# A transformer block on one core: weight differences made once and kept in DRAM, in place of being remade at each use

## The chip, the core and the metric

The kernel runs on one core of a Trainium2 chip. Its engines run side by side and meet through semaphores: TensorE (PE: matrix products and transposes), VectorE (DVE), ScalarE (ACT), GpSimd (POOL) and SyncE (SP), whose queue issues almost all transfers between DRAM and the on-chip memory. The metric is the device time of one execution in microseconds (us), lower is better. A change of under 0.2% cannot be told from none here.

## What is computed

64 sequences of 64 positions and 256 features go through four layers: cross attention with a gate (L0), cross attention with 16 heads and a GELU feed-forward block (L1), and two layers (2 and 3) that have two sets of weights each, `v` and `l`. A mask `vm` chooses per position which set is used. The change is in their feed-forward blocks:

```python
vm = expert_mask(token_type_ids)[..., None]      # True where this and the next type are 1
mi = rms_norm(hidden_states, ln_post_attn_w)
v_out = silu(mi @ v_gate) * (mi @ v_up) @ v_down
l_out = silu(mi @ l_gate) * (mi @ l_up) @ l_down
hidden_states = hidden_states + where(vm, v_out, l_out)
```

The weights are 256 x 688 (gate, up) and 688 x 256 (down), float32.

## The kernel before

**The product with a difference.** For every position the kernel multiplies by `l`, and adds the product of `v - l` with the activations masked by `vm`: where the mask is 0 the second part vanishes, where it is 1 it turns `l` into `v`. For this input only positions 48 to 63 of a sequence have a mask that can be 1 (`late`, a branch chosen on the chip at the start), so the second product covers 128 of 512 columns.

**Groups, streams, turns.** The 64 sequences make 8 groups of 512 positions. Two groups are in work at once, stream a (0) and stream b (1), and there are 4 turns of two groups. While one stream is in attention, which has long chains over all engines, the other is in a feed-forward block, which is mostly TensorE work. At the very end stream b's last feed-forward block has nothing beside it.

**The feed-forward steps.** 688 hidden features are 6 tiles (`j` 0 to 5, five of 128 and one of 48). A tile has the steps `g` (gate product, PE; lines 1358 and 1364), `silu` (DVE and POOL), `u` (up product, the same lines, then DVE 1817 to 1837 and POOL) and `down` (lines 1375, 1385).

**The ring.** The weights of a tile (a chunk: 768 KB, `l` and `v` of gate, up and down) are loaded anew at each use into one of 5 slots of `w_ring`, by six transfers on SP's queue (lines 937 to 939). GELU chunks (`f1`) use the same ring. A slot is reloaded when the last product of its chunk is done. There are 96 feed-forward chunks: 4 turns x 2 streams x 2 layers x 6.

**The step `weigh`.** After a chunk has landed, GpSimd turns its `v` part into `v - l` in place: three subtractions (line 1908 twice, line 1909), and PE's `g` waits for the third. GpSimd also normalises the attention's probabilities (`prob`, line 1861), builds block-diagonal keys (1891, 1899), and takes a part in the rotation (`rot`, 1884) and in the masks (1878, 1916, 1924).

**The planner.** The order of steps on each engine is computed when the kernel is built: `schedule` takes the steps in a nominal order (`global_order`), and puts next the one that could start first by its table of assumed costs (`parts`), by what it must follow (`follows`), and by the free banks and ring slots (`room`). Each engine then runs its list strictly in order. Where the plan leaves PE idle before a step, `PAUSES` gives a number of filler products (line 982: a 128x512 bf16 product into the bank that the step will overwrite), issued in the step's place in the order, before the step's own waits. SP's order (`transfers`) is by planned time too.

**The norm.** RMS norms take their reciprocal root on DVE by nine dependent operations on 128x2 or 128x4 elements (lines 1711 to 1731); the step `spread` (PE, line 1217) waits for the last.

Of the kernel before, what the change touches and what calls it, by code (L numbers as in the profile page):

```python
# [163 lines left out]


def attention_lane(n):
    return q_stage(n)[0] + [(when + q_stage(n)[1], *step) for when, *step in attention_stage(n)[0]]


def global_order():  # L170
# [22 lines left out]
    then((1, TURNS - 1, finish, (0, 0), (3, 3)))  # L193
    return order

# [150 lines left out]


def accumulation(token):

    return token[:3] + (token[3:4] if token[0] == "down" else ())  # L350
# [7 lines left out]
def schedule(nominal):  # L358
# [33 lines left out]
    def inputs(token):  # L392
        if token not in ready_at:
            step, s, turn, *where = token
            latest = 0.0
            for engine, t, name, *at in follows(step, turn, where):
                other = (name, s if name != "table" else 0, t, *at)
                when = over.get(other) if engine is None else end.get((other, engine))
                if when is None:
                    return None  # L400
                latest = max(latest, when)
            ready_at[token] = latest
        return ready_at[token]
# [8 lines left out]
    def room(token):  # L412
# [3 lines left out]
        if step == "weigh":  # L416
            return slot()
        if step == "l1h" and where[0] % 2 == 0:
            there, free = slot(), banks(1)
            return None if there is None or free is None else max(there, free)  # L420
# [52 lines left out]
    while True:  # L473
# [26 lines left out]
        if pieces[k][2] is None and token not in orders_set:  # L500

            orders_set.add(token)
            heads[step, s].pop()
            if step == "weigh":
                chunks.append((("ffn", s, turn, *where), ("down", s, turn, *where)))
            if step == "l1h" and where[0] % 2 == 0:
                chunks.append((("f1", s, turn, where[0] // 2), ("w2", s, turn, where[0] + 1)))
            for j, (other, _, follow) in enumerate(pieces):
                if follow is None and j != k:
                    waiting.setdefault(key_of(step, s, other), []).append((token, j, at))  # L510
# [54 lines left out]
def transfers():  # L565

    found = [(BEGIN[token, "SP"], token) for token in ORDER["SP"] if token[0] == "store" or token[2]]
    for chunk, n in CHUNKS.items():
        found.append((END[CHUNK_ENDS[n - SLOTS], "PE"] if n >= SLOTS else -1.0, ("chunk", *chunk)))
    return [token for _, token in sorted(found, key=lambda v: v[0])]  # L570

# [49 lines left out]
def xattn_kernel(nc, a, out):  # L621
    ctx = ExitStack()

    def sb(name, shape, dt=F32):
# [132 lines left out]
    g_ready, th_ready, silu_ready, h_ready = (pair(name, 2 * FT) for name in ("g_ready", "th_ready", "silu_ready", "h_ready"))  # L757
    weighed, sv_ready, hv_late, hv_early, down_done = (pair(name, 2 * FT) for name in ("weighed", "sv_ready", "hv_late", "hv_early", "down_done"))
    w_weighed = sem("w_weighed")
    out_ready = pair("out_ready", 2)  # L760
# [73 lines left out]
    def sums(token):  # L834

        return [banks[BANK["sum", m, accumulation(token)]] for m in range(DT)]

    def chunk(*key):

        n = CHUNKS[key]  # L840
        count = sum(16 * (2 if c[0] == "f1" else 6) for c, m in CHUNKS.items() if m <= n and m % SLOTS == n % SLOTS)
        return w_ring[:, n % SLOTS, :], (chunk_loaded[n % SLOTS], count)

    def f1_weights(ring):
        return (ring[:, 0:512].rearrange("p (k n) -> p k n", k=DT), ring[:, 512:1024].rearrange("p (t d) -> p t d", t=2))

    def ffn_weights(ring):
# [46 lines left out]
    with nc.Block() as block:  # L894
        @block.sync
        def _(q):
# [20 lines left out]
            def load_chunk(*key):  # L917
                ring, _ = chunk(*key)
                n = CHUNKS[key]
                if n >= SLOTS:  # L920
                    step, s, turn, *where = CHUNK_ENDS[n - SLOTS]
                    if step == "w2":
                        q.wait_ge(*w2_done[s].at(turn, where[0] + 1))
                    else:
                        q.wait_ge(*down_done[s].at(turn, FT * (where[0] - 2) + where[1] + 1))
                here = chunk_loaded[n % SLOTS]
                if key[0] == "f1":
# [7 lines left out]
                into, down = ffn_weights(ring)  # L935
                for e in "lv":
                    q.dma_start(into["g"][e][:, :, 0:rows], tiles(a[f"L{layer}_{e}_gate"])[:, :, j * P:j * P + rows]).then_inc(here, 16)
# [24 lines left out]
            for step, *where in ORDER["SP"][SLOTS:]:  # L962
                if step == "load":
                    load(*where)
                elif step == "chunk":
                    load_chunk(*where)
                elif step == "store":
                    s, turn = where
# [3 lines left out]
            for s in range(STREAMS):  # L972
                q.wait_ge(*stored[s].at(TURNS, 0))

        @block.tensor
        def _(pe):
# [150 lines left out]
            def stages(every):  # L1127
                for token in ORDER["PE"]:
# [212 lines left out]
                    if step in ("g", "u"):  # L1341
                        n, j = where
                        rows = P if j < FT - 1 else FR
                        ring, _ = chunk("ffn", s, turn, n, j)
# [501 lines left out]
        def _(pool):  # L1846
# [3 lines left out]
            for token in ORDER["POOL"]:  # L1850
# [49 lines left out]
                if step == "weigh":  # L1900
# [8 lines left out]
                    G_.tensor_tensor(down["v"][0:rows, :], down["v"][0:rows, :], down["l"][0:rows, :], ALU.subtract).then_inc(weighed[s].sem, 1)  # L1909
                if step == "silu":  # L1910
# [57 lines left out]
```

## Time and profile before

| | us |
|---|---|
| median of 3 runs | 2689.42 (2686.3 to 2690.03) |
| the profiled execution: time | 2684.68 |
| its span, first to last instruction | 2682.8 |
| PE busy | 2560.8, 95% |
| DVE busy | 1534.7, 57% |
| ACT busy | 1222.7, 46% |
| POOL busy | 1155.9, 43% |
| transfers, mean | 41 GB/s |

The mean granted TensorE clock is 0.993 of full. Busy time of PE includes the filler products. Times within the span are from its start. The turns begin at about 0, 660, 1318 and 1977 us.

### The profile page before, as it was taken

The page shows a single profiled execution, that of the slowest core. Times are in us where ns is not written, and L with a number is a line of the kernel's source. Part 1 is how long each engine was busy: PE and PEld are TensorE (multiplying, and loading weights), DVE is VectorE, ACT ScalarE, POOL GpSimd, SP SyncE. Part 2 cuts the span into 40 slices and gives each one's busy share as a digit, 9 for nine tenths or more (in the row PEclk, how much of TensorE's full clock was granted, in tenths as well). Part 3 has the DMA queues.
Part 4 walks back from the last instruction along what each step waited for, and adds up shares of the span by engine and source line. Part 5 has one row for each costly group of instructions (what it writes and reads, how often), then busy time and mean ns, then how long its engine had stood idle before and what let it go on. Part 6 is the DMA issues. An engine that isn't in the chain of part 4 may idle for free.

```text
span 2682.8 us, 54240 instructions
## 1 busy us (share of the span) xinstructions
PE 2560.8 (95%) x20342; PEld 1554.7 (58%) x20342; DVE 1534.7 (57%) x3448; ACT 1222.7 (46%) x4274; POOL 1155.9 (43%) x1242
## 2 busy tenths in 40 slices
PE   6999999999999999999999999999999999999998
PEld 3556556665565656566555565665656556566565
DVE  2537556766434646776644464677644456467763
ACT  2335444644333635464433362654544346265462
POOL 0025265665211527656410342765641034267564
PEclk9999999999999999999999999999999999999999
DMA  8010011112201011121220101112121000120211
GB/s 211 1 32 2 22 44 48 41 41 72 72 2 32 2 41 40 32 58 31 70 68 1 32 2 52 38 28 60 29 72 60 9 25 2 52 60 10 55 41 44
DMA packets 171100, 109.61 MB, mean 41 GB/s; under 512 B 31764, under 2 KB 168408, under 8 KB 170712
## 3 DMA queue, kind: packets, MB, share of 16 engines
q1 hardware_dynamic: 166384, 105.82, 14.2%
q8 instruction: 167, 2.74, 0.4%
q10 hardware_dynamic: 4456, 0.29, 0.2%
q14 instruction: 93, 0.76, 0.1%
HBM read 101.87 MB, written 4.19 MB: 40 GB/s over the span
## 4 chain that ended last, share of the span: by engine, by line
PE 82%; DVE 11%; POOL 2%; issue 2%; ACT 1%; ACTq 1%; DMA 0%; SPq 0%; DVEq 0%
PE bank L1358 10%; PE bank L1375 6%; PE bank L1081 6%; PE bank L995 5%; PE bank L1244 4%; PE bank L1251 4%; PE bank L1263 4%; PE bank L1272 4%; PE bank L1364 3%; PE bank L1116 2%; PE bank L1298 2%; PE bank L1098 2%; PE bank L1057 2%; PE bank L1224 2%; PE bank L1070 2%
## 5 line engine op out<-in xcount | busy, mean ns | idle before, releaser
L1861 POOL TENSOR_TENSOR Ebuf<-Ebuf,row_rcp 128x512 f32<-128x512 f32 (+1 forms) x328 | 345.8, 1060 | 797.4 <-DVE row_rcp L1684 796.3
L1463 ACT ACTIVATE Ebuf<-bank,minus_max 128x64 f32<-128x64 f32 x1312 | 392.4, 334 | 39.8 <-DVE minus_max L1668 39.5
L1668 DVE TENSOR_REDUCE minus_max<-bank 128x8 f32<-128x512 f32 (+1 forms) x328 | 219.8, 673 | 161.2 <-PE bank L1070 81.2
L1463 ACT ACTIVATION_READ_ACCUMULATOR Ebuf<-bank,minus_max 128x1 f32 x1312 | 297.4, 227 | 0.0
L1472 ACT ACTIVATE PT<-bank 128x512 f32<-128x512 f32 (+1 forms) x328 | 192.6, 601 | 152.5 <-PE bank L1081 151.0
L1081 PE MATMUL bank<-ident,Ebuf 128*128 128x128 f32 x1296 | 201.5, 283 | 9.9 <-POOL Ebuf L1861 9.4
L1081 PEld LDWEIGHTS bank<-ident,Ebuf 128*128 128x128 f32 x1296 | 146.4, 143 | 64.5 <-issue 39.2
L1358 PE MATMUL bank<-xs_a,w_ring 128*128 128x512 f32 (+1 forms) x384 | 172.2, 611 | 7.7 <-POOL w_ring L1909 7.3
L1358 PE MATMUL bank<-xs_b,w_ring 128*128 128x512 f32 (+1 forms) x384 | 169.1, 602 | 5.9 <-POOL w_ring L1909 3.9
L1456 ACT ACTIVATE Ebuf<-Ebuf 128x512 f32<-128x512 f32 x160 | 102.0, 638 | 101.6 <-DVE Ebuf L1673 99.5
L1908 POOL TENSOR_TENSOR w_ring<-w_ring 128x256 f32<-128x256 f32 x192 | 131.9, 708 | 0.0
L1673 DVE TENSOR_TENSOR Ebuf<-bank,minus_max 128x512 f32<-128x512 f32 x160 | 110.7, 692 | 16.9 <-DVE minus_max L1668 0.5
L1682 DVE TENSOR_REDUCE row_sum<-Ebuf 128x8 f32<-128x512 f32 x160 | 107.9, 675 | 8.6 <-ACT Ebuf L1456 7.8
L982 PE MATMUL bank<-causal_bf,ident_bf 128*128 128x512 bf16 x414 | 109.3, 384 | 0.0
L1684 DVE RECIPROCAL row_rcp<-row_sum 128x8 f32<-128x8 f32 (+1 forms) x328 | 65.4, 200 | 70.6 <-ACT Ebuf L1463 64.5
L1358 PEld LDWEIGHTS bank<-xs_a,w_ring 128*128 128x128 f32 (+1 forms) x384 | 59.4, 180 | 67.7 <-issue 65.1
L1358 PEld LDWEIGHTS bank<-xs_b,w_ring 128*128 128x128 f32 (+1 forms) x384 | 59.1, 179 | 66.6 <-issue 64.3
L1375 PE MATMUL bank<-arena_a,w_ring 128*128 128x512 f32 (+1 forms) x192 | 94.2, 613 | 1.7 <-DVE arena_a L1833 1.7
L1375 PE MATMUL bank<-arena_b,w_ring 128*128 128x512 f32 (+1 forms) x192 | 92.9, 606 | 2.7 <-DVE arena_b L1833 2.7
L1878 POOL TENSOR_TENSOR xs_a<-xs_a,masks_a 128x192 f32<-128x192 f32 (+1 forms) x48 | 36.2, 774 | 133.4 <-DVE xs_a L1745 133.4
L1817 DVE SCALAR_TENSOR_TENSOR arena_b<-arena_b 128x512 f32<-128x512 f32 (+1 forms) x48 | 42.7, 889 | 76.2 <-ACT arena_b L1581 76.0
L1899 POOL TENSOR_TENSOR arena_b<-arena_b,head_rows 128x512 f32<-128x512 f32 x64 | 65.5, 1056 | 42.5 <-PE bank L1070 28.9
(325 smaller groups left out, 5599.6 us busy)
## 6 DMA issues: line engine op xcount, KB each, us to landing
w_ring<-in_L_W SPq DMA_DIRECT2D x64, 256.0 KB, 3.0
w_ring<-in_L_l_gate SPq DMA_DIRECT2D x80, 128.0 KB, 2.2
w_ring<-in_L_l_up SPq DMA_DIRECT2D x80, 128.0 KB, 2.3
w_ring<-in_L_l_down SPq DMA_DIRECT2D x80, 128.0 KB, 2.2
w_ring<-in_L_v_gate SPq DMA_DIRECT2D x80, 128.0 KB, 2.4
w_ring<-in_L_v_up SPq DMA_DIRECT2D x80, 128.0 KB, 2.4
w_ring<-in_L_v_down SPq DMA_DIRECT2D x80, 128.0 KB, 2.5
arena_a<-in_x SPq DMA_DIRECT2D x4, 512.0 KB
```

Source lines behind the costliest of these rows:

```text
L982: mm(b[:, :].rearrange("p (h s) -> p h s", h=8), ident_bf[:, :], causal_bf[:, :].unsqueeze(1).broadcast_to([P, 8, S]), start=True, stop=True)
L995: mm(b, w_l[k], src_l[k], start=(k == 0), stop=(not every and k == DT - 1))
L1081: last = nc.tensor.transpose(b[:, c * P:(c + 1) * P], Ebuf[:, u % UNITS, c * P:(c + 1) * P], ident[:, :])
L1358: mm(to, of["l"][:, k, 0:rows], st.xn[:, k, :], start=(k == 0), stop=(not every and k == DT - 1))
L1375: mm(acc[m][:, :], w["l"][0:rows, m * P:(m + 1) * P], st.hid_l[0:rows, j % 2, :], start=(j == 0), stop=(not every and j == FT - 1), skip_g ...
L1463: last = A(Ebuf[:, u % UNITS, cell], bank(token)[:, cell], ACT.Exp, bias=minus_max[:, u % UNITS, c:c + 1], accum_out=row_sum[:, u % UNITS, ...
L1472: A(PT[:, t % 2, 0:width(key) * S], bank(token)[:, 0:width(key) * S], ACT.Copy).then_inc(pt_ready, 1)
L1668: V.reduce_max(minus_max[:, u % UNITS, 0:g], cells(bank(token)[:, 0:g * S]), AX_X, negate=True).then_inc(maxed, 1)
L1673: V.tensor_tensor(cells(Ebuf[:, u % UNITS, 0:g * S]), cells(bank(token)[:, 0:g * S]), minus_max[:, u % UNITS, 0:g].unsqueeze(2).broadcast_ ...
L1682: V.reduce_sum(row_sum[:, u % UNITS, 0:g], cells(Ebuf[:, u % UNITS, 0:g * S]), AX_X).then_inc(summed, 1)
L1861: G_.tensor_tensor(v, v, row_rcp[:, n % 3, 0:g].unsqueeze(2).broadcast_to([P, g, S]), ALU.mult).then_inc(probs_ready, 1)
L1908: G_.tensor_tensor(rare, rare, other, ALU.subtract)
```

## The change

`weigh` stays only for the first use of each chunk: stream a, turn 0, layers 2 and 3, 12 of 96. After it SP's queue writes the differences of that chunk to a DRAM tensor `differences` (step `keep`). Every later use loads `l` by three transfers as before, and the three differences by one transfer of 384 KB (three for the 48-row tile), and PE's `g` waits for these transfers themselves. A load of a difference waits until its `keep` has landed, and a slot whose difference is being kept is not reloaded before. The planner drops the other 84 `weigh` steps, and claims the ring slot of such a chunk when it places `g`.

```diff
+def first_use(token):
+    return token[1:3] == (0, 0)
...
-    return order
+    return [(when, token) for when, token in order if token[0] != "weigh" or first_use(token)]
...
+def begins_chunk(token):
+    return token[0] == "g" and not first_use(token) or token[0] == "l1h" and token[3] % 2 == 0
...
             for engine, t, name, *at in follows(step, turn, where):
+                if name == "weigh" and not first_use(token):
+                    continue
...
-        if step == "l1h" and where[0] % 2 == 0:
+        if begins_chunk(token):
             there, free = slot(), banks(1)
...
-            if step == "weigh":
-                chunks.append((("ffn", s, turn, *where), ("down", s, turn, *where)))
             if step == "l1h" and where[0] % 2 == 0:
                 chunks.append((("f1", s, turn, where[0] // 2), ("w2", s, turn, where[0] + 1)))
+            elif step == "weigh" or begins_chunk(token):
+                chunks.append((("ffn", s, turn, *where), ("down", s, turn, *where)))
...
+    for token in ORDER["POOL"]:
+        if token[0] == "weigh":
+            found.append((END[token, "POOL"], ("keep", *token[1:])))
     return [token for _, token in sorted(found, key=lambda v: v[0])]
...
+    scratch = nc.dram_tensor("differences", (2 * FT, P, 3, DT * P), F32).ap()
...
+    kept = [sem(f"kept{k}") for k in range(SLOTS)]
...
+                    if step == "down" and first_use(CHUNK_ENDS[n - SLOTS]):
+                        q.wait_ge(*kept_at(*where))
...
-                for e in "lv":
+                if not first_use(key):
+                    q.wait_ge(*kept_at(layer, j))
+                    for dst, src in zip(rarer(rare_share(ring), j), rarer(scratch[FT * (layer - 2) + j], j)):
+                        q.dma_start(dst, src).then_inc(here, 16)
+                for e in "lv" if first_use(key) else "l":
                     q.dma_start(into["g"][e][:, :, 0:rows], ...).then_inc(here, 16)
...
+                elif step == "keep":
+                    n, j = where[2:]
+                    ring, _ = chunk("ffn", *where)
+                    q.wait_ge(weighed, FT * (n - 2) + j + 1)
+                    for dst, src in zip(rarer(scratch[FT * (n - 2) + j], j), rarer(rare_share(ring), j)):
+                        q.dma_start(dst, src).then_inc(kept_at(n, j)[0], 16)
...
                         if step == "g":
-                            pe.wait_ge(*weighed[s].at(turn, FT * (n - 2) + j + 1))
+                            pe.wait_ge(*((weighed, FT * (n - 2) + j + 1) if first_use(token) else there))
```

The planner's orders change with this. The lines of the changed kernel are 51 higher in this part of the file: 1358 becomes 1409, 1364 becomes 1415, 982 becomes 1033.

PE, second turn, the start of stream a's feed-forward block of layer 2. L1298 is stream b's value projection of layer 2; L1358 and L1364 with `xs_a` are one gate or up product. Before, around the gate product of tile 1:

```order
L1298 MATMUL bank7<-w2_l_qkv,xs_b 128x256 x2
L1298 MATMUL bank7<-w2_v_qkv,xs_b 128x256 x2
L1358 MATMUL bank4<-xs_a,w_ring 128x512 x2
L1364 MATMUL bank4<-xs_a,w_ring 128x8x16 x2
L1298 MATMUL bank0<-w2_l_qkv,xs_b 128x256 x2
L1298 MATMUL bank0<-w2_v_qkv,xs_b 128x256 x2
```

The same product now, the second of the two that stand first:

```order
L1409 MATMUL bank3<-xs_a,w_ring 128x512 x2
L1415 MATMUL bank3<-xs_a,w_ring 128x8x16 x2
L1409 MATMUL bank4<-xs_a,w_ring 128x512 x2
L1415 MATMUL bank4<-xs_a,w_ring 128x8x16 x2
L1259 MATMUL bank7<-ones,sq 128x1 x4
L1033 MATMUL bank2<-causal_bf,ident_bf 128x512 x2
L1409 MATMUL bank2<-xs_a,w_ring 128x512 x2
L1415 MATMUL bank2<-xs_a,w_ring 128x8x16 x2
```

Gate 1 has moved from between stream b's value projections to right behind gate 0, ahead of stream b's norm (L1259).

PE, last turn, the start of stream b's last feed-forward block; L982 is the filler. Before:

```order
L982 MATMUL bank2<-causal_bf,ident_bf 128x512 x4
L1358 MATMUL bank2<-xs_b,w_ring 128x512 x2
L1364 MATMUL bank2<-xs_b,w_ring 128x8x16 x2
L982 MATMUL bank0<-causal_bf,ident_bf 128x512 x6
L1358 MATMUL bank0<-xs_b,w_ring 128x512 x2
L1364 MATMUL bank0<-xs_b,w_ring 128x8x16 x2
L1358 MATMUL bank5<-xs_b,w_ring 128x512 x2
L1364 MATMUL bank5<-xs_b,w_ring 128x8x16 x2
```

The same place now:

```order
L1033 MATMUL bank3<-causal_bf,ident_bf 128x512 x4
L1409 MATMUL bank3<-xs_b,w_ring 128x512 x2
L1415 MATMUL bank3<-xs_b,w_ring 128x8x16 x2
L1409 MATMUL bank1<-xs_b,w_ring 128x512 x2
L1415 MATMUL bank1<-xs_b,w_ring 128x8x16 x2
L1033 MATMUL bank0<-causal_bf,ident_bf 128x512 x2
L1409 MATMUL bank0<-xs_b,w_ring 128x512 x2
L1415 MATMUL bank0<-xs_b,w_ring 128x8x16 x2
```

Six fillers between gate 0 and gate 1 are gone, two came ahead of the up product. Over the whole branch that this input takes, the fillers go from 414 to 385: by turn 118, 92, 94, 110 before, and 111, 93, 94, 87 now.

POOL, second turn, beside the first place: the rotation of stream b (`cos_sin`) and its keys (`head_rows`). Before:

```order
L1884 TENSOR_TENSOR arena_b<-arena_b,cos_sin 128x512 x3
L1908 TENSOR_TENSOR w_ring<-w_ring 128x256 x2
L1909 TENSOR_TENSOR w_ring<-w_ring 128x256
L1884 TENSOR_TENSOR arena_b<-arena_b,cos_sin 128x512
L1891 TENSOR_TENSOR arena_b<-arena_b,head_rows 128x2x256 x2
L1908 TENSOR_TENSOR w_ring<-w_ring 128x256 x2
L1909 TENSOR_TENSOR w_ring<-w_ring 128x256
```

Now:

```order
L1929 TENSOR_TENSOR xs_b<-xs_b,masks_b 128x8x48 x2
L1975 TENSOR_TENSOR arena_a<-arena_a,masks_a 128x8x48
L1935 TENSOR_TENSOR arena_b<-arena_b,cos_sin 128x512 x4
L1942 TENSOR_TENSOR arena_b<-arena_b,head_rows 128x2x256 x6
L1912 TENSOR_TENSOR Ebuf<-Ebuf,row_rcp 128x512
```

The subtractions on `w_ring` stood between the rotation and the keys, and are gone.

## Rows read from the trace of the kernel before

**Rows 1.** The page, parts 1 and 4: busy time; the chain that ended last.

```profile
PE 2560.8 (95%) x20342; PEld 1554.7 (58%) x20342; DVE 1534.7 (57%) x3448; ACT 1222.7 (46%) x4274; POOL 1155.9 (43%) x1242
...
PE 82%; DVE 11%; POOL 2%; issue 2%; ACT 1%; ACTq 1%; DMA 0%; SPq 0%; DVEq 0%
```

**Rows 2.** Busy time by stretch, the second turn and the last.

```profile
core 0: us, PE busy (x) PEld busy (x) DVE busy (x) ACT busy (x) POOL busy (x), PEclk, DMA share, GB/s
660.00:1318.00 658.00, 635.65 (x5073) 387.05 (x5072) 383.04 (x856) 305.38 (x1068) 286.47 (x309) 0.99 0.14 38
1977.00:2683.00 706.00, 676.80 (x5248) 409.19 (x5246) 394.50 (x876) 314.32 (x1083) 304.14 (x336) 1.00 0.13 37
```

**Rows 3.** Waits of PE: who for whom, us in total, times, longest.

```profile
PE bank L1217 <- DVE norm_a L1731: 25.3, 18, 2.0
PE bank L1217 <- DVE norm_b L1731: 20.4, 20, 2.6
PE bank L1358 <- POOL w_ring L1909: 11.2, 8, 1.8
PE bank L1081 <- POOL Ebuf L1861: 9.4, 9, 2.1
```

**Rows 4.** Timeline of PE, last turn: start, length, engine, line, work.

```profile
2637.42 1.46 PE L982 MATMUL bank<-causal_bf,ident_bf 128*128 128x512 bf16 x6
2638.72 1.88 PE L1358 MATMUL bank<-xs_b,w_ring 128*128 128x512 f32 x4
...
2640.88 1.45 PE L1358 MATMUL bank<-xs_b,w_ring 128*128 128x512 f32 x3
```

**Rows 5.** Timeline of POOL and PE, second turn, around gate product 1.

```profile
1020.76 1.86 POOL L1908 TENSOR_TENSOR w_ring<-w_ring 128x256 f32<-128x256 f32 x2
1022.59 1.17 POOL L1909 TENSOR_TENSOR w_ring<-w_ring 128x256 f32<-128x256 f32 x1
...
1023.90 1.96 PE L1358 MATMUL bank<-xs_a,w_ring 128*128 128x512 f32 x4 [1.84 <-POOL w_ring L1909]
```

**Rows 6.** Groups by line, POOL: the subtractions of `weigh`.

```profile
L1908 POOL TENSOR_TENSOR w_ring<-w_ring 128x256 f32<-128x256 f32 x192 | 131.9, 708 | 0.0
L1909 POOL TENSOR_TENSOR w_ring<-w_ring 128x256 f32<-128x256 f32 x96 | 73.4, 764 | 0.0
```

**Rows 7.** Timelines of DVE, POOL, PE, second turn: one norm's chain.

```profile
1266.07 0.65 DVE L1724 TENSOR_TENSOR norm_b<-norm_b 128x2 f32<-128x2 f32 x1
...
1267.43 0.65 DVE L1728 SCALAR_TENSOR_TENSOR norm_b<-norm_b 128x2 f32<-128x2 f32 x1
1268.12 0.16 DVE L1731 SCALAR_TENSOR_TENSOR norm_b<-norm_b 128x2 f32<-128x2 f32 x1
...
1265.98 1.41 POOL L1908 TENSOR_TENSOR w_ring<-w_ring 128x256 f32<-128x256 f32 x2
1267.34 0.73 POOL L1909 TENSOR_TENSOR w_ring<-w_ring 128x256 f32<-128x256 f32 x1
...
1268.43 0.40 PE L1217 MATMUL bank<-ident,norm_b 128*128 128x128 f32 x2 [2.63 <-DVE norm_b L1731]
```

**Rows 8.** Timeline of DVE, second turn: first and last of 23 slowed ones.

```profile
1102.52 0.56 DVE L1714 TENSOR_SCALAR norm_b<-norm_b 128x2 int32<-128x2 int32 x1
...
1303.35 0.65 DVE L1721 SCALAR_TENSOR_TENSOR norm_b<-norm_b 128x2 f32<-128x2 f32 x1
```

**Rows 9.** Timelines of SP and PE, last turn: the last chunk, loaded and used.

```profile
2647.99 0.37 SPq L937 DMA_DIRECT2D w_ring<-in_L_l_gate  x1
...
2665.62 1.92 PE L1358 MATMUL bank<-xs_b,w_ring 128*48 128x512 f32 x8
```

**Rows 10.** Transfers: count, size, median us from issue to landing.

```profile
w_ring<-in_L_W SPq DMA_DIRECT2D x64, 256.0 KB, 3.0
...
out_x<-arena_a SPq DMA_DIRECT2D x4, 512.0 KB, 4.1
w_l_qkv<-in_L_l_qkv SPq DMA_DIRECT2D x2, 768.0 KB, 6.6
```

More of the change, by code:

```diff
@@ L757, in xattn_kernel @@
     g_ready, th_ready, silu_ready, h_ready = (pair(name, 2 * FT) for name in ("g_ready", "th_ready", "silu_ready", "h_ready"))
-    weighed, sv_ready, hv_late, hv_early, down_done = (pair(name, 2 * FT) for name in ("weighed", "sv_ready", "hv_late", "hv_early", "down_done"))
-    w_weighed = sem("w_weighed")
+    sv_ready, hv_late, hv_early, down_done = (pair(name, 2 * FT) for name in ("sv_ready", "hv_late", "hv_early", "down_done"))
+    w_weighed, weighed = sem("w_weighed"), sem("weighed")
+    kept = [sem(f"kept{k}") for k in range(SLOTS)]
     out_ready = pair("out_ready", 2)
@@ L836, in sums, with loads, kept_at, rarer @@
         return [banks[BANK["sum", m, accumulation(token)]] for m in range(DT)]
+    def loads(key):
+        return 2 if key[0] == "f1" else 6 if first_use(key) or key[4] == FT - 1 else 4
+    def kept_at(n, j):
+        m = CHUNKS["ffn", 0, 0, n, j]
+        before = [c for c, k in CHUNKS.items() if c[0] == "ffn" and first_use(c) and k <= m and k % SLOTS == m % SLOTS]
+        return kept[m % SLOTS], sum(16 * (3 if c[4] == FT - 1 else 1) for c in before)
+    def rarer(v, j):
+        if j < FT - 1:
+            return [v]
+        return [v[:, m, :].rearrange("p (k n) -> p k n", k=DT)[:, :, 0:FR] for m in range(2)] + [v[0:FR, 2, :]]
     def chunk(*key):
         n = CHUNKS[key]
-        count = sum(16 * (2 if c[0] == "f1" else 6) for c, m in CHUNKS.items() if m <= n and m % SLOTS == n % SLOTS)
+        count = sum(16 * loads(c) for c, m in CHUNKS.items() if m <= n and m % SLOTS == n % SLOTS)
         return w_ring[:, n % SLOTS, :], (chunk_loaded[n % SLOTS], count)
@@ L845, in f1_weights, with rare_share @@
         return (ring[:, 0:512].rearrange("p (k n) -> p k n", k=DT), ring[:, 512:1024].rearrange("p (t d) -> p t d", t=2))
+    def rare_share(ring):
+        return ring.rearrange("p (a e c) -> p a e c", a=3, e=2)[:, :, 1, :]
     def ffn_weights(ring):
@@ L973, in _ @@
                 q.wait_ge(*stored[s].at(TURNS, 0))
+            for n in (2, 3):
+                for j in range(FT):
+                    q.wait_ge(*kept_at(n, j))
         @block.tensor
@@ L1343, in stages @@
                         rows = P if j < FT - 1 else FR
-                        ring, _ = chunk("ffn", s, turn, n, j)
+                        ring, there = chunk("ffn", s, turn, n, j)
                         w = ffn_weights(ring)[0][step]
@@ L1908, in _ @@
                         G_.tensor_tensor(rare, rare, other, ALU.subtract)
-                    G_.tensor_tensor(down["v"][0:rows, :], down["v"][0:rows, :], down["l"][0:rows, :], ALU.subtract).then_inc(weighed[s].sem, 1)
+                    G_.tensor_tensor(down["v"][0:rows, :], down["v"][0:rows, :], down["l"][0:rows, :], ALU.subtract).then_inc(weighed, 1)
                 if step == "silu":
```

## Prediction

> **What bounds the kernel now.** I read the page first. PE is busy 95% of the span and holds 82% of the chain that ended last; POOL is busy 43% and holds 2% of that chain [rows 1]. So GpSimd's load as such is no bound, and what is taken from it counts only where PE waits for it. The table of stretches comes second: in the second turn PE is busy 635.65 of 658.00 us, which leaves 22.35 us idle [rows 2]. Third, PE's waits: 45.7 us for the last operation of the norm's chain on DVE, in 38 places, 11.2 us for `weigh` in 8 places, 9.4 us for the probabilities of GpSimd [rows 3]. Busy time of PE also hides waiting: where the plan expects a wait it puts filler products. From the timeline of PE, six of them start at 2637.42 and the product behind them at 2638.72, so one costs 1.30 / 6 = 0.217 us [rows 4]. The 414 fillers are 90 us of planned waiting that no wait row shows.
>
> The working is against the profiled execution, 2684.68 us (span 2682.8 and 1.9 around it). The median of the three runs is 4.74 us above it, so a sum on it is carried over to the median by adding 4.74. Under 0.2%, 5.4 us, is no change that a measurement of this kernel can tell.
>
> **What is removed.** 84 of 96 `weigh` steps go. The groups of POOL give 131.9 + 73.4 = 205.3 us for all [rows 6], so 205.3 x 84 / 96 = 180 us less of GpSimd: 976 us busy, 36% of the span. That is no gain by itself. Three things follow from it on PE.
>
> (a) The fillers. The new order has 385, 29 fewer, and they are instructions that PE issues whether anybody is late or not: 29 x 0.217 = 6.3 us [rows 4]. Of the 29, 23 go in the last turn and 7 in the first, where before each gate product 1 the plan had allowed for GpSimd; in the second and third turn the count goes up by one and stays. Whether a removed filler is a gain depends on what PE does next: in the last turn the six ahead of gate 1 [rows 4] are followed by a gate product whose inputs are long there, so PE moves up at once, and only the up product behind it got two. I take 6.3. Its ends are 0 (all turn into idle time) and 6.3.
>
> (b) The waits for `weigh`. In the second turn PE stood 1.84 us before gate product 1, until the third subtraction was done; the three took 1.86 + 1.17 us [rows 5]. All 8 such waits sum to 11.2 us, the longest 1.8 [rows 3]. The first turn's, for stream a's layer 2, is a first use and stays with its 1.8; 9.4 us can go. What is late next there is GpSimd's own rotation and the keys of the other stream, which PE's scores need: they stood behind the subtractions and now move up by their 3 us too, so that the next wait doesn't simply take the place. I take half of it, 4.7 us, since the moved gate product uses up PE work that covered stream b's norm before; the ends are 0 and 9.4.
>
> (c) DVE behind GpSimd. The nine small operations of a norm take 0.16 us each when nothing else runs. In the second turn, at 1266 us, three of them take 0.65 each while three subtractions on `w_ring` run, and the next, behind the subtractions, takes 0.16 again; PE stood 2.63 us for this chain [rows 7]. So one `weigh` cost 3 x (0.65 - 0.16) = 1.5 us of that wait. In the whole second turn 23 such operations, from 1102.52 to 1303.35, ran slow with a subtraction beside them, in 7 chains [rows 8]. I take one such place of 1.5 us in each of the last three turns as a gain, 4.5 us; the other chains end under fillers or under work. The ends: 0 (no operation on DVE gets longer by GpSimd's leaving), and 7 chains x 1.5 x 3 = 31, which the 45.7 us of PE's waits for norms [rows 3] would hold, but only with every chain on PE's path; I count a third, 10.
>
> The Trainium skill, page SBUF — State Buffer, section "Who interferes with whom", says that VectorE with two inputs in SBUF contends with a GpSimd instruction that reads SBUF, by an exclusive lock. A reader without it would price (c) at nothing, and the sum would be 4.5 us less. The trace agrees with the rule: 0.65 against 0.16 us [rows 7].
>
> **What is added.** 12 writes of 384 KB in the first turn, on the queue of SP. A write of 512 KB landed in 4.1 us [rows 10]. Behind a `keep` that waits for GpSimd stand chunk loads on that queue, and PE waits for those; the tightest chunk is the last one of the last turn, whose first transfer was issued at 2647.99 and which was used at 2665.62, 17.6 us later [rows 9]. A `keep` is planned at the end of its subtraction, so its wait is what GpSimd is late against the plan, a few us at most against 17: cost 0, ends 0 and 3 us.
>
> PE now waits for the landing of the transfers. The difference is one of 384 KB: between a transfer of 256 KB in 3.0 us and one of 768 KB in 6.6 [rows 10]. With four issues of about 0.5 us, against six before, it is all there 5 to 9 us after the first issue, of 17.6: cost 0. Bytes per chunk stay as they were. The two waits on `kept` are on things long past, but for the first turn: 0.
>
> **What is moved.** Every order is new. The largest move is that gate product 1 now follows gate 0 at once and stands ahead of part of the other stream's projections and scores. PE's work is the same, so this costs only what it delays elsewhere: 0 as likeliest, and rival D for the other end.
>
> **The sum.** 6.3 + 4.7 + 4.5 = 15.5 us. 2684.68 - 15.5 = 2669.2, and as a median 2673.9 us, 2674.
>
> **Rivals.**
>
> B, only the plan's own waits go: the fillers' 6.3 us, while (b) and (c) come back as waits for the chains of DVE and ScalarE behind. For it: PE's waits for DVE's norms are four times those for `weigh` [rows 3]. Against: the 2.63 us with subtractions beside the chain [rows 7]. 2684.68 - 6.3 + 4.74 = 2683.1 us.
>
> C, nothing moves: the second and third turn keep 92 to 94 fillers, and the last turn's removed fillers become idle time before the up product, which needs DVE's work. For it: POOL holds 2% of the chain [rows 1]. Against: PE follows its list strictly and has 22 us of idle time per turn to lose [rows 2]. About 2689 us.
>
> D, slower: the early gate product starves the other stream. Each turn has four feed-forward blocks; in each the other stream's scores stand one product later, 2.16 us (from the start of one at 2638.72 to that of the next at 2640.88 [rows 4]). Their softmax chain goes over DVE, ScalarE and GpSimd before PE can transpose, and starts that much later. In the last three turns that is 12 x 2.16 = 26 us, less the 15.5 gained: 10.5 slower, 2700 us. The point from which it decides: when PE has no other work to put under the chain's end, so that its idle time per turn goes from 22.35 us [rows 2] to above 27.5 (22.35 + 15.5 / 3). Against it: the list puts up to four products of the block between the scores and their use, and the products that came early are not needed later.
>
> E, more of the same: all 9.4 us of (b), a third of (c)'s end, 10, and the fillers' 6.3 are 25.7, with 2 us for GpSimd's probabilities, which PE awaited for 9.4 [rows 3]: 27.7 less, 2661.7 us.
>
> That the change doesn't do what it says (GpSimd still subtracting, or PE waiting for a late landing) would show as 2690 or more; the 17.6 us of lead [rows 9] leave it little, and I count it with D.
>
> **How the numbers follow.** Forecast 50% (its own range 2667 to 2681), B 20%, C 12%, D 8%, E 10%. The bound of faster is 2689.42 - 5.4 = 2684.0: the forecast, E and three fifths of B are under it, 72%; the rest of B and C are within, 20%; D is slower, 8%. The range goes from E's 2662 to C's 2689: D, what of C lies above, and what of E lies below are 2 in 10.
>
> **What would show it.** POOL busy near 976 us. PE's waits for w_ring's subtraction only in the first turn, under 3 us. PE's waits for the norms' last operation down from 45.7 to about 41, and DVE's operations on 128x2 back at 0.16 us in most places. Filler products 385. Turns two and three 3 to 5 us shorter than 658, the last turn 6 to 8 shorter than 706. No wait of PE for a transfer into `w_ring`. Wrong would be: turns two and three as long as before (then (b) and (c) were given back: B or C), PE's idle time per turn up (D), or a PE wait for a transfer of the differences.

## The result and the profile after

The changed kernel takes 2657.61 us (median of 4 runs, 2651.89 to 2662.27) against 2689.73 for the one before (4 runs, 2686.3 to 2692.01), a ratio of 0.9881 [0.9858, 0.9904]: 32 us faster. The forecast was 2674, 15.5 us faster, in a range from 2662 to 2689. The direction was right, the gain twice as large as forecast and outside the range.

The page of the changed kernel, parts 1 (busy us, share of the span, instructions) and 4 (the chain that ended last, by engine), against [rows 1]:

```profile
PE 2555.1 (96%) x20313; PEld 1545.3 (58%) x20313; DVE 1508.8 (57%) x3448; ACT 1224.6 (46%) x4274; POOL 985.4 (37%) x990
...
PE 84%; DVE 10%; issue 2%; ACT 2%; POOL 1%; ACTq 1%; DVEq 0%
```

GpSimd lost 170.5 us of busy time, where 180 were forecast. DVE's busy time fell with it: the same 3448 instructions take 1508.8 us, where before they took 1534.7. Nothing that DVE computes was changed. The 25.9 us are near the 31 that the prediction gave as the end of (c), so what it had wrong is not how much DVE is held up, but how much of that reaches PE.

PE's waits in the changed kernel (who for whom: us in total, times, longest), to be laid beside [rows 3] (the changed kernel's lines here lie 51 further down):

```profile
PE bank L1268 <- DVE norm_a L1782: 22.0, 18, 2.0
...
PE bank L1268 <- DVE norm_b L1782: 9.9, 17, 1.2
...
PE bank L1409 <- POOL w_ring L1960: 1.8, 1, 1.8
```

The waits for the norms fell from 45.7 to 31.9 us, those for `weigh` from 11.2 to 1.8. No wait of PE for a transfer into `w_ring` came in their place. All waits of PE sum to 92.4 us, against 115.5 before. Of the 28.8 us by which the profiled span is shorter (2682.8 and 2654.0) these are 23.1, and PE's busy time, with 29 fillers less, gives the other 5.7.

Busy time by stretch, cut where stream a's output is first read, once per turn. The same marks lie at 655.69, 1313.72, 1973.12 and 2631.73 us in the kernel before, 658.03 and 659.40 us for the second and third turn:

```profile
core 0: us, PE busy (x) PEld busy (x) DVE busy (x) ACT busy (x) POOL busy (x), PEclk, DMA share, GB/s
652.42:1296.61 644.19, 631.23 (x5033) 382.89 (x5034) 372.09 (x853) 305.04 (x1066) 235.89 (x236) 0.99 0.14 40
1296.61:1944.55 647.94, 633.38 (x5077) 384.18 (x5074) 374.01 (x856) 305.86 (x1068) 236.59 (x237) 1.00 0.13 39
1944.55:2654.00 709.45, 685.25 (x5279) 411.42 (x5276) 392.51 (x891) 317.34 (x1087) 248.62 (x251) 0.99 0.13 37
```

The second and third turn are 13.8 and 11.5 us shorter, where 3 to 5 were forecast. The last turn, from its mark to the end of the span, takes 709.45 us against 709.68 before (2682.80 - 1973.12). It gained nothing, although 6 to 8 us were forecast and 23 of the 29 removed fillers stood in it. The split by turns depends on the mark, since the new order also shifts the two streams against each other: by the transfers of stream b's output, the first comes 9.5 us earlier, and the stretches to the second, third and fourth are 3.2, 10.6 and 5.4 us shorter. The granted clock is within 0.01 of that in [rows 2].

A norm's chain of the changed kernel, second turn: timelines of DVE and of GpSimd (start us, us, line, operation). It is the same step as in [rows 7]:

```profile
1250.39 0.16 DVE L1768 TENSOR_TENSOR norm_b<-norm_b 128x2 f32<-128x2 f32 x1
...
1251.56 0.16 DVE L1782 SCALAR_TENSOR_TENSOR norm_b<-norm_b 128x2 f32<-128x2 f32 x1
...
1249.41 0.91 POOL L1975 TENSOR_TENSOR arena_a<-arena_a,masks_a 128x384 f32<-128x384 f32 x1
1251.60 2.04 POOL L1950 TENSOR_TENSOR arena_b<-arena_b,head_rows 128x512 f32<-128x512 f32 x2 [1.27 <-ACT arena_b L1598]
```

The operations run at 0.16 us with GpSimd idle beside them, and no wait of PE for this chain is left. Part of that is the new order: in the kernel before, three more operations of this chain, from 1263.08 us on, took 0.96 us each beside the building of keys, and here the keys come later.

What was added, by the groups of transfers (KB each, median us from issue to landing):

```profile
w_ring<-differences SPq DMA_DIRECT2D x70, 384.0 KB, 3.5
...
w_ring<-in_L_l_gate SPq DMA_DIRECT2D x80, 128.0 KB, 3.3
...
differences<-w_ring SPq DMA_DIRECT2D x10, 384.0 KB, 2.9
```

and by the waits of SP's queue (for whom: us in total, times, longest):

```profile
SPq L1014 <- POOL w_ring L1960: 147.4, 9, 103.7
```

The `keep` steps held SP's queue for 147.4 us in 9 places, once for 103.7. All of it is in the first turn, and no wait of PE for a transfer shows behind it. I had taken "a few us at most" for one such wait: wrong by far, and of no consequence.

### The profile page after: what moved, and what is told of

Same layout as the page of the kernel before. It is cut to its first block, busy times and chain, and to the rows that moved or that the text cites. A ratio compares the mean times of both kernels' runs of the same rounds, so it can differ in the third digit from the quotient of the medians.

```text
span 2654.0 us, 53911 instructions
## 1 busy us (share of the span) xinstructions
PE 2555.1 (96%) x20313; PEld 1545.3 (58%) x20313; DVE 1508.8 (57%) x3448; ACT 1224.6 (46%) x4274; POOL 985.4 (37%) x990
## 4 chain that ended last, share of the span: by engine, by line
PE 84%; DVE 10%; issue 2%; ACT 2%; POOL 1%; ACTq 1%; DVEq 0%
PE bank L1409 11%; PE bank L1426 6%; PE bank L1046 6%; PE bank L1132 5%; PE bank L1302 4%; PE bank L1295 4%; PE bank L1314 4%; PE bank L1323 4%; PE bank L1349 3%; PE bank L1415 3%; PE bank L1108 2%; PE bank L1149 2%; PE bank L1275 2%; PE bank L1167 2%; PE bank L1286 2%
## 5 line engine op out<-in xcount | busy, mean ns | idle before, releaser
L1033 PE MATMUL bank<-causal_bf,ident_bf 128*128 128x512 bf16 x385 | 101.6, 381 | 0.0
L1259 PEld LDWEIGHTS bank<-ones,sq 128*128 128x128 f32 x576 | 73.9, 191 | 15.0 <-issue 9.9
L1950 POOL TENSOR_TENSOR arena_a<-arena_a,head_rows 128x512 f32<-128x512 f32 x64 | 65.3, 1048 | 40.4 <-PE bank L1121 32.0
```

## The experiments

**Theories.** After the result I had two. *Reads*: GpSimd's subtractions lengthen DVE's operations beside them, and these stand on PE's path far more often than forecast. *Order*: the new order of steps, with its early gate product and 29 fillers fewer, brings the gain. Behind them stand two smaller ones: the direct wait for the third subtraction, and the time that the subtractions take in GpSimd's queue, whatever they read. Runs of one paragraph shared a chip with the kernel before; each ratio is against the kernel before on that chip.

### The data path alone, and the order alone

`e1_old_order` has the changed data path (12 subtractions, the rest loaded as differences), but PE, DVE and ScalarE keep the order of the kernel before, with its 414 fillers:

```diff
-    return [(when, token) for when, token in order if token[0] != "weigh" or first_use(token)]
+    return order
...
-        if begins_chunk(token):
+        if step == "l1h" and where[0] % 2 == 0:
...
-                if step == "weigh":
+                if step == "weigh" and first_use(token):
```

> The changed kernel's data path (84 subtraction steps gone, differences loaded from DRAM), with PE, DVE and ACT in the order of the kernel before and its 414 fillers. The measured gain of the whole change is 32 us. Theory 1 (the subtractions themselves held PE up, by being awaited and by holding DVE's small operations): waits of PE for the subtraction fall by 9.4 us, those for the norms from 45.7 to about 32, no filler is saved, so 32 less 7: about 25 us faster, 2665. Rival (the new order made the gain): only the 9.4 us of direct waits, partly given back, 5 to 9 us faster, 2681 to 2685.

`e2_new_order` is the reverse: the kernel before with its 96 subtractions, and the order that the change gives to PE, DVE and ScalarE, 385 fillers. The subtractions stand in GpSimd's list before the gate product's planned time:

```diff
+def with_weighing():
+    lead = 9.0
+    found = [(BEGIN[token, "POOL"], 1, token) for token in ORDER["POOL"]]
+    for chunk, n in CHUNKS.items():
+        token = ("weigh", *chunk[1:])
+        if chunk[0] == "ffn" and not first_use(token):
+            freed = END[CHUNK_ENDS[n - SLOTS], "PE"] if n >= SLOTS else 0.0
+            found.append((max(freed + LOADED, BEGIN[("g", *chunk[1:]), "PE"] - lead), 0, token))
...
```

> The data path of the kernel before (96 subtraction steps on GpSimd, nothing written to DRAM), with PE, DVE and ACT in the new order and its 385 fillers; GpSimd subtracts as early as 9 us ahead of the gate product in the plan. Theory 1: only the fillers are saved and the norms' waits stay near 45 us, so 6 to 8 us faster, 2682 to 2684, or less if the subtraction comes late before a gate product. Rival (the order made the gain): 20 to 25 us faster, 2665 to 2670, with the norms' waits near 32 us although the subtractions run.

Measured: `e1_old_order` 2651.57 us, 0.9869 [0.9846, 0.9892]; `e2_new_order` 2712.88 us, 1.0096 [1.0074, 1.0117]. The data path alone gives all of the gain, the order alone, with the subtractions where I placed them, makes the kernel 26 us slower (0.0096 of 2689). *Reads* had put the first at 2665, 13 us too slow, and the second at 6 to 8 us faster, which is the wrong way. PE's waits in `e1_old_order`:

```profile
PE bank L1266 <- DVE norm_a L1780: 19.0, 13, 2.0
PE bank L1266 <- DVE norm_b L1780: 9.5, 15, 1.2
PE bank L1130 <- POOL Ebuf L1910: 9.4, 9, 2.1
```

and in `e2_new_order`:

```profile
PE bank L1244 <- DVE norm_a L1758: 26.9, 18, 2.6
PE bank L1244 <- DVE norm_b L1758: 23.4, 20, 2.6
PE bank L1108 <- POOL Ebuf L1888: 16.6, 25, 2.1
```

The norms wait less only where the subtractions are gone, and GpSimd's probabilities are awaited for 9.4 us in the one and 16.6 in the other. For a subtraction PE waits only 1.8 us in `e2_new_order`, so without the direct wait, but with the reads, nothing is gained there. *Order* is refuted as the source of the gain.

### Subtractions that nobody waits for, and writes that read nothing

Both kernels are `e1_old_order` with work put back on GpSimd in the place of each removed step. `e3_idle_subtract` makes three subtractions of the old shapes from a resident weight tile into a spare tile, nobody waits for them:

```diff
+                if step == "weigh" and not first_use(token):
+                    rows, wide = (P, D) if where[1] < FT - 1 else (FR, 2 * FR)
+                    for r, w in ((P, wide), (P, wide), (rows, D)):
...
+                        G_.tensor_tensor(spare[0:r, spared % 2, 0:w], w_mem[0:r, 0:w], w_mem[0:r, 0:w], ALU.subtract).then_inc(spare_done, 1)
```

> The old order with the differences loaded from DRAM, and in the place of each of the 84 steps GpSimd does three subtractions of the same shapes on tiles that nobody waits for (both inputs are a constant weight tile). What it leaves of the old kernel is GpSimd's time and its reads, without the wait of PE for the result. If the wait itself was the cost, it is as fast as the old order without subtractions (about 2665 by theory 1). If GpSimd's reads beside DVE and its later steps being late are the cost, the norms' waits are back near 45 us and the time is 2675 to 2681: only the direct waits, 9.4 us, are saved.

`e4_idle_fill` puts memsets of 128x512 there, which read nothing from the on-chip memory:

```diff
+                    for _ in range(4 if where[1] < FT - 1 else 3):
...
+                        G_.memset(spare[:, :], 0.0).then_inc(spare_done, 1)
```

> As the run with idle subtractions, but with memsets of about the same total length per step (four, or three for the short tile, of 128x512), which read nothing. The lock theory (DVE is held by GpSimd's reads): DVE's small operations take 0.16 us beside them, the norms' waits are near 32 us and the time is within 4 us of the old order without subtractions. The queue theory (GpSimd's own later steps, keys, masks and probabilities, come late behind whatever it does): as slow as with idle subtractions.

Measured: `e3_idle_subtract` 2689.33 us, 1.0007 [0.9993, 1.0022]; `e4_idle_fill` 2658.71 us, 0.9893 [0.9873, 0.9913]. The first was expected at 2675 to 2681 if reads cost, and is slower still; the second within 4 us of `e1_old_order`, and is 6.5 us slower by the ratios, with intervals that overlap. The page's part 1 for `e3_idle_subtract`:

```profile
PE 2560.5 (95%) x20342; PEld 1554.2 (58%) x20342; DVE 1537.6 (57%) x3448; ACT 1221.9 (46%) x4274; POOL 1126.8 (42%) x1242
```

its group of idle subtractions on GpSimd (busy us, mean ns):

```profile
L1958 POOL TENSOR_TENSOR spare<-w_mem 128x256 f32<-128x256 f32 x210 | 130.0, 645 | 0.0
```

its waits of PE:

```profile
PE bank L1268 <- DVE norm_a L1782: 23.7, 17, 2.0
PE bank L1268 <- DVE norm_b L1782: 20.0, 22, 2.3
PE bank L1359 <- DVE Ebuf L1724: 10.1, 3, 3.4
```

and its timelines of DVE, GpSimd and PE at the chain of [rows 7]:

```profile
1264.64 0.54 DVE L1775 TENSOR_TENSOR norm_b<-norm_b 128x2 f32<-128x2 f32 x1
...
1262.56 2.04 POOL L1952 TENSOR_TENSOR arena_b<-arena_b,head_rows 128x512 f32<-128x512 f32 x2
1264.55 1.75 POOL L1958 TENSOR_TENSOR spare<-w_mem 128x256 f32<-128x256 f32 x3
...
1266.66 0.59 PE L1268 MATMUL bank<-ident,norm_b 128*128 128x128 f32 x2 [2.29 <-DVE norm_b L1782]
```

The same four views of `e4_idle_fill`, the page:

```profile
PE 2558.1 (96%) x20342; PEld 1553.0 (58%) x20342; DVE 1503.6 (57%) x3448; ACT 1222.0 (46%) x4274; POOL 1147.9 (43%) x1312
```

the memsets:

```profile
L1957 POOL MEMSET spare<- 128x512 f32 x322 | 169.2, 525 | 13.7
```

PE's waits:

```profile
PE bank L1269 <- DVE norm_a L1783: 21.5, 18, 2.0
PE bank L1269 <- DVE norm_b L1783: 9.9, 16, 1.2
```

and the timelines:

```profile
1258.69 0.16 DVE L1776 TENSOR_TENSOR norm_b<-norm_b 128x2 f32<-128x2 f32 x1
...
1258.57 1.69 POOL L1957 MEMSET spare<- 128x512 f32 x3
...
1259.58 0.40 PE L1269 MATMUL bank<-ident,norm_b 128*128 128x128 f32 x2 [1.17 <-DVE norm_b L1783]
```

GpSimd is as busy in `e4_idle_fill` as before the change, and even more than in `e3_idle_subtract`; still only the subtractions cost. DVE's operation beside one of them takes 0.54 us, beside a memset 0.16, and PE's wait at this place doubles from 1.17 to 2.29 us. *Reads* holds. The Trainium skill says, in SBUF — State Buffer, section "Who interferes with whom", that a DVE instruction with two inputs in SBUF contends with a GpSimd instruction that reads SBUF, and not with one that only writes it. The trace agrees: 0.54 us against 0.16.

Both kernels have the new data path, and with idle subtractions it takes as long as the kernel before, so the path by itself is no rival for a gain of this size. From `e3_idle_subtract` to `e4_idle_fill` only subtractions are exchanged for memsets, and the time falls by 30.7 us (0.0114 x 2689).

But `e3_idle_subtract` is no fair copy of the old subtractions. Its wait of PE at line 1359, 10.1 us in three places, exists nowhere in the kernel before, and leaves about 20 of the 30.7 us. The timelines of DVE and GpSimd ahead of the first of them, of `e3_idle_subtract`

```profile
1038.05 5.88 DVE L1868 SCALAR_TENSOR_TENSOR arena_a<-arena_a 128x512 f32<-128x512 f32 x2 [1.03 <-ACT arena_a L1632]
...
1036.03 3.04 POOL L1914 TENSOR_TENSOR Ebuf<-Ebuf,row_rcp 128x512 f32<-128x512 f32 x3
1039.04 2.03 POOL L1944 TENSOR_TENSOR arena_b<-arena_b,head_rows 128x512 f32<-128x512 f32 x2
1041.03 1.74 POOL L1958 TENSOR_TENSOR spare<-w_mem 128x256 f32<-128x256 f32 x3
```

and of the kernel before, the same step:

```profile
1041.72 0.69 DVE L1817 SCALAR_TENSOR_TENSOR arena_a<-arena_a 128x512 f32<-128x512 f32 x1 [1.03 <-ACT arena_a L1581]
1042.96 0.90 DVE L1817 SCALAR_TENSOR_TENSOR arena_a<-arena_a 128x512 f32<-128x512 f32 x1 [0.55 <-ACT arena_a L1581]
...
1041.78 2.98 POOL L1891 TENSOR_TENSOR arena_b<-arena_b,head_rows 128x512 f32<-128x512 f32 x2
```

In the one, two wide operations take 5.88 us together, until after GpSimd's run of eight instructions without a gap. In the other they take 0.69 and 0.90, and it is GpSimd that is held: 2.98 us for two instructions of about 1.0. DVE started 0.06 us ahead of these two instructions there, and in the middle of GpSimd's run here. The Trainium skill says, in SBUF — State Buffer, section "Who interferes with whom", that the order of issue decides who is held. The two rows agree, and no run varied it by itself. So a kernel was needed with the waits and the queue of the kernel before, but without the reads.

### The same queue and the same wait, without the reads

`e7_fill_awaited` is `e4_idle_fill`, and the gate product waits for its memsets as it waited for the subtractions. Beside the path of the weights, which `e3_idle_subtract` has too, that leaves as difference to the kernel before the subtractions' reads (and their writes, which memsets of about the same total length stand for):

```diff
+                            if not first_use(token):
+                                pe.wait_ge(spare_done, FILLED["weigh", s, turn, n, j])
```

> The old order with the differences loaded from DRAM, memsets in the place of the 84 subtraction steps, and each gate product waits for the last memset of its chunk, as it did for the subtraction: the direct wait without GpSimd's reads. Theory (the direct wait is worth nothing by itself; GpSimd's reads beside DVE were the whole cost): within 3 us of the run with memsets that nobody awaits (2658.7). Rival (the wait counts where DVE is not held up too): up to 9.4 us slower than that, 2668, with a wait of PE for GpSimd of some 10 us in 7 or 8 places.

`e8_idle_copy` is `e3_idle_subtract` with copies, one input instead of two:

```diff
-                        G_.tensor_tensor(spare[0:r, spared % 2, 0:w], w_mem[0:r, 0:w], w_mem[0:r, 0:w], ALU.subtract).then_inc(spare_done, 1)
+                        G_.tensor_copy(spare[0:r, spared % 2, 0:w], w_mem[0:r, 0:w]).then_inc(spare_done, 1)
```

> As the run with idle subtractions that nobody awaits, but each is a copy with one input read from SBUF in place of two. Theory (any GpSimd instruction that reads SBUF holds DVE's two-input operations, for its whole length): DVE busy near 1530 us, the norms' waits above 38 us, and 15 to 30 us slower than the run with memsets, 2675 to 2689, less if a copy is shorter than a subtraction. Rival (only the second read costs): as the run with memsets, 2659.

Measured: `e7_fill_awaited` 2664.58 us, 0.9909 [0.9893, 0.9926]; `e8_idle_copy` 2656.65 us, 0.9885 [0.9868, 0.9901]. `e7_fill_awaited` is slower than `e4_idle_fill` by 4.3 us (ratios) or 5.9 (medians): above the theory's 3, within the rival's 9.4 and with the rival's waits in 7 places, but the intervals overlap, so neither is excluded. For `e8_idle_copy` the theory's 2675 to 2689 failed, and the rival's 2659 came near. PE's waits in `e7_fill_awaited`:

```profile
PE bank L1273 <- DVE norm_a L1789: 21.5, 18, 2.0
PE bank L1273 <- DVE norm_b L1789: 11.0, 17, 1.2
...
PE bank L1416 <- POOL spare L1963: 7.8, 7, 1.4
```

Two of DVE's groups there (busy us, mean ns):

```profile
L1875 DVE SCALAR_TENSOR_TENSOR arena_b<-arena_b 128x512 f32<-128x512 f32 x40 | 30.6, 764 | 73.6 <-ACT arena_b L1639 73.5
L1836 DVE TENSOR_TENSOR xs_b<-bank,masks_b 128x256 f32<-128x256 f32 x64 | 25.5, 414 | 5.5 <-PE bank L1163 5.4
```

The same two groups in the kernel before:

```profile
L1817 DVE SCALAR_TENSOR_TENSOR arena_b<-arena_b 128x512 f32<-128x512 f32 x40 | 35.8, 896 | 71.8 <-ACT arena_b L1581 71.7
L1778 DVE TENSOR_TENSOR xs_b<-bank,masks_b 128x256 f32<-128x256 f32 x64 | 25.5, 414 | 5.5 <-PE bank L1107 5.4
```

With GpSimd's queue as full as before and 9.6 us of direct waits (7.8, and the first turn's 1.8) in place of 11.2, the kernel is still 24.5 us faster (0.0091 x 2688.4; 19.9 to 28.8). DVE is busy 1502.1 us in place of 1534.7. Nearly all of that difference is in the operations on `norm` (the 128x2 ones fall from 162.4 to 142.7 us over all groups) and in the rotation's on `arena`, most of which read two operands from the on-chip memory. A group that has one operand in a bank takes 25.5 us in both kernels.

In `e8_idle_copy` the chain reads, timelines of DVE and GpSimd:

```profile
1256.96 0.30 DVE L1775 TENSOR_TENSOR norm_b<-norm_b 128x2 f32<-128x2 f32 x1
...
1256.85 1.08 POOL L1958 COPY spare<-w_mem 128x256 f32<-128x256 f32 x3
```

A copy with one input holds DVE too, but only for its own 1.08 / 3 = 0.36 us. All the copies have 52 us less of GpSimd's time than the subtractions of `e3_idle_subtract` (1074.4 against 1126.8 us busy), and the kernel is no slower than the one with memsets. DVE is busy 1515.5 us, 11.9 above `e4_idle_fill`, and PE's waits for the norms are 33.8 us against 31.4. So reads that take 88 us of GpSimd's time (1074.4 against 986.6 in `e1_old_order`) cost nothing that these runs can tell, and reading alone does not set the price. What of this is the shorter duration and what the missing second input, this run doesn't separate.

### The fillers

Four kernels on one chip, with the kernel before at 2689.49 us. `e1_again` and `after_again` are `e1_old_order` and the changed kernel once more. `e5_no_gate_fill` is `e1_old_order` without the 40 fillers that stand ahead of gate products 1, where the old plan allowed for `weigh`:

```diff
-                if token not in BEFORE_TABLE:
+                if token not in BEFORE_TABLE and not (token[0] == "g" and token[4] == 1):
```

`e6_no_fill` is the changed kernel without any of its 385:

```diff
-                    for _ in range(PAUSES[token]):
+                    for _ in range(0):
```

> The old order with the differences loaded from DRAM, once more, as the base on this chip for the three others. Both theories: 0.985 to 0.990 of the kernel before, near 2651 us.

> The changed kernel as it is, beside the old order on the same chip. Theory 1 as it stood in the forecast (the 29 fillers that the new order saves are a gain of 6.3 us): it must be some 6 us faster than the old order, near 2645. Rival (the new order and its fillers are worth nothing, or cost a little, and the whole gain is GpSimd's reads being gone): the same as the old order or up to 6 us slower, 2651 to 2658.

> The old order with the differences loaded from DRAM, without the 40 filler products ahead of gate product 1, which had been put there for the wait for GpSimd's subtraction (374 fillers are left). If a filler that covers no wait costs its 0.217 us: 8.7 us faster than the old order, near 2643. If PE meets the next wait earlier instead, by the same time: 0 to 3 us faster.

> The changed kernel without any of its 385 fillers, 84 us of products. If fillers only stand in time that PE would wait anyway: within 5 us of the changed kernel, as long as the granted clock stays at 0.99. If some of them delay PE's own work: up to 20 us faster, 2637. If the idle time that they cover costs TensorE its clock: slower, with a granted clock under 0.99, 2665 or more.

| kernel | us | ratio |
|---|---|---|
| `e1_again` | 2653.76 | 0.9871 [0.985, 0.9891] |
| `after_again` | 2658.31 | 0.9888 [0.9868, 0.9907] |
| `e5_no_gate_fill` | 2645.79 | 0.9849 [0.9832, 0.9867] |
| `e6_no_fill` | 2702.57 | 1.0053 [1.0035, 1.0071] |

Taking 40 fillers away gave 8.0 us by the medians where 40 x 0.217 = 8.7 were expected. By the ratios it is 5.9, and the intervals overlap, but the slowest run of `e5_no_gate_fill` (2649.64) is faster than the fastest of `e1_again` (2651.33). It is the fastest kernel of this study. `after_again` is not near 2645, so the forecast's gain from the 29 fillers failed; it lies at the rival's slow end. Taking all away costs 44.3 us. Busy time and granted clock (the column behind POOL's) of stretches of 3 us in the first turn of `e6_no_fill`:

```profile
312.00:315.00 3.00, 2.01 (x17) 1.73 (x12) 2.08 (x6) 0.87 (x2) 0.00 (x0) 1.00 0.00 0
315.00:318.00 3.00, 1.59 (x8) 1.62 (x8) 1.86 (x9) 1.49 (x2) 0.00 (x0) 0.54 0.00 0
318.00:321.00 3.00, 1.31 (x3) 0.73 (x4) 2.77 (x11) 0.00 (x0) 0.00 (x0) 0.50 0.00 0
321.00:324.00 3.00, 3.00 (x7) 1.33 (x6) 0.32 (x2) 0.38 (x1) 0.00 (x0) 0.50 0.00 0
```

PE idles 1.0, 1.4 and 1.7 us of the first three, the clock falls from 1.00 to 0.50, its lower level of 1.2 GHz, and is still there while PE works through the fourth. Of 880 such stretches 86 are below 0.9, in the changed kernel 17, and the mean is 0.957 against 0.993. The waits for the norms grew too, from 31.9 to 48.5 us: what is no longer filled is waited for, and more besides. So the fillers hold the clock, as a whole; which of them do is open, but for the 40.

## Why the prediction was wrong in size

The runs make a chain. Its first step exchanges the subtractions for memsets and brings the new data path, and each later one differs by one thing; in us against the kernel before (ratio x 2689):

| kernel | what goes | ratio | us |
|---|---|---|---|
| `e7_fill_awaited` | the reads | 0.9909 | -24.5 |
| `e4_idle_fill` | the direct wait too | 0.9893 | -28.8 |
| `e1_old_order` | GpSimd's time too | 0.9869, 0.9871 | -35.2, -34.7 |
| changed kernel | and the new order | 0.9881, 0.9888 | -32.0, -30.1 |

The intervals reach 4 to 6 us to either side. So the first step is shown; of the later ones only the sum from `e7_fill_awaited` to `e1_old_order` is (10.7 us), not its parts.

**Step (c), DVE behind GpSimd, failed.** The rule was the right one, the row [rows 7] was the right one, and the size was 4.5 us where 24.5 were measured. Its upper end of 31 held, but I drew the range with a third of it. "I take one such place of 1.5 us in each of the last three turns as a gain, 4.5 us; the other chains end under fillers or under work" was an assumption with no row behind it. In `e7_fill_awaited` DVE's operations on `norm` are 24.0 us shorter (19.7 in those on 128x2, 4.3 in those on 128x4), and PE's waits for the norms 45.7 - 32.5 = 13.2 us: more than half of what DVE lost in these chains showed in PE's waits, not one chain in seven. These 13.2 us are what the rows place. The two profiled executions differ by 19.3 us (2682.8 and 2663.5), and where the rest of the 24.5 lies is open. A filler shelters a chain only as long as it lasts, and it is issued however late the chain is. Nor were the small operations of [rows 8] all: the wide ones of the rotation, which I didn't price, were held for 5.2 us in the group of stream b shown above.

**Step (b), the direct wait.** 4.7 us taken, ends 0 and 9.4. From `e7_fill_awaited` to `e4_idle_fill` the ratio falls by 0.0016, 4.3 us, and the medians, from two chips, by 5.9. The size agrees, as far as intervals that overlap can say. Whether a direct wait is given back elsewhere while DVE is held is open: in `e3_idle_subtract` PE's waits sum to 114.6 us, against 115.5 before, but 10.1 of them are the wait that only this kernel has.

**GpSimd's time in its queue** was no term of the sum, "no gain by itself". From `e4_idle_fill` to `e1_old_order` 0.0024, 6.5 us, and the intervals overlap.

**Step (a), the fillers.** The count of 385 was right, and the price of one agrees with the 8.0 us of the 40. Yet the kernel with 29 fewer is not 6.3 us faster than `e1_old_order`, but 4.6 slower on the same chip (2658.31 against 2653.76, intervals overlapping). If the 29 are worth their 6.3 us, the order that came with them costs about 11, where the prediction put the moves at 0 and only rival D gave them a cost. D's mechanism doesn't show, though. It wanted PE idle for more than 27.5 us a turn, and the second and third turn have 13.0 and 14.6.

In `e2_new_order` the cost lies in the last turn. Between the third and the fourth transfer of stream a's output it takes 681.4 us, the kernel before 658.6, which is 22.8 of the 26 us. Its granted clock is lower there too: 0.98 between 1979 and 2640 us, against 1.00 before. Over its six runs the mean clock is 0.984 to 0.989, against 0.987 to 0.995 in the 17 of the kernel before. For the same stretch the changed kernel takes 659.7 us in both of its traces, and `e1_old_order` and `e1_again` take 649.8 and 655.3. Why the new order is slow there, and what of it is the clock, I haven't shown. E's size, 27.7, came nearest of the rivals'.

**The checks.** POOL 985.4 us (976 forecast), fillers 385, the wait for `w_ring` 1.8 us in one place, and no wait for the transfers: right. The 17.6 us of lead [rows 9] covered landings that took 3.3 us where 2.2 was usual before for such a transfer. The norms' waits went to 31.9 us, not to 41, and the second and third turn became 14 and 12 us shorter, not 4: the first points at (c), the second at (b) and (c). The last turn was to be 6 to 8 us shorter and gained nothing, which points at (a).

So the sum that would have come out is 24.5 + 4.3 + 6.5 less 3 to 5 for the order, about 31.

## What to carry to other kernels

Price work on GpSimd also by what it reads from the on-chip memory while DVE works on two operands there, not only by its load or by what waits for it. Reading alone doesn't set it: copies of 0.36 us each cost nothing here that could be told. When rows show an operation three or four times as long beside it, let the range reach all the places in the trace unless a row shows where the lateness ends. Before a large transformation test it with cheap kernels: the removed work left in its place but idle, and memsets in its place, with the wait and without. The first against the second gives the price of the reads, as long as no new wait comes in, so look for one. Then look at fillers or pauses that the old plan had put in for the removed step, since they don't go by themselves, but test which of them hold the clock before taking more.

## What the runs showed of the hardware

- A DVE operation with two inputs of 128x2 elements takes 0.16 us alone, and beside a GpSimd instruction that reads about as long as that one: 0.96 beside instructions of 128x512 (1.02 us; at 1263 us in the kernel before), 0.65 and 0.54 beside subtractions of 128x256 (0.71 and 0.58), 0.30 beside copies (0.36), but 0.16 beside memsets (0.56). In these rows one gets in per GpSimd instruction, so a chain of small ones is held once for each.
- A wide one can be held for longer: two operations of 0.69 us took 5.88 together beside GpSimd's run of eight without a gap. Where they had started just ahead of two of GpSimd's instructions, they took 0.69 and 0.90, and GpSimd 2.98 for two of about 1.0.
- The fillers, 385 x 0.217 = 84 us of them, are worth more than they cost: without them the mean granted clock falls from 0.993 to 0.957 of full speed, and the time rises by 44.3 us.
- Writing 384 KB to DRAM landed in 2.9 us and reading it back in 3.5.
